# One fused attention block on one core: self attention's lead in another order, and one small exponential ahead of two leads

## The reference

```python
# layer 0: 8 heads of 40, keys and values from 1020 context rows, and a small extra attention
out = (mha(x @ Wq, enc @ Wk, enc @ Wv) + ca_hs2) @ Wout + b_out + x
# layer 1: 20 heads of 16
h1 = ln(x);  x = attn(h1, h1)      @ o1_w + o1_b + x     # self attention, 512 keys
h2 = ln(x);  x = attn(h2, context) @ o2_w + o2_b + x     # cross attention, 1024 keys
h3 = ln(x);  a, g = split(h3 @ ff_w1 + ff_b1);  x = a * gelu(g) @ ff_w2 + ff_b2 + x
# attn: softmax(q k^T * scale) v, exact to fp32, with the row's maximum taken off first
```

## Time and profile before

| | us |
|---|---|
| median of 3 runs | 864.62 |
| lowest and highest | 861.23 to 865.34 |
| the profiled execution, its own time | 866.39 |
| its span, first to last instruction | 864.6 |
| self attention's lead, first maximum on PE to first scores | 315.85 to 342.97 |

### The profile page before, as it was taken

How to read it: one execution, slowest core, us unless ns; L and a number is a source line. 1 busy time by engine, 2 the same in 40 slices (tenths; PEclk the granted TensorE clock), 3 DMA queues, 4 the chain that set the end, 5 groups by cost and what they waited for, 6 DMA issues and landing times.

```text
span 864.6 us, 11612 instructions
## 1 busy us (share of the span) xinstructions
PE 813.4 (94%) x4172; PEld 448.9 (52%) x4172; DVE 585.0 (68%) x1104; ACT 488.0 (56%) x744; POOL 121.4 (14%) x201
## 2 busy tenths in 40 slices
PE   5899999999999998999999889999999999899998
PEld 3777644444466665333335553333333333678888
DVE  4454576777685547599966468999999962684231
ACT  4643454554543632576777676777667777863130
POOL 5100103100005342000004500000000000540000
PEclk9998999999999998599999959999999999999999
DMA  8986478522301184122116512222222000500000
GB/s 289 283 280 212 135 219 258 149 85 67 122 15 57 33 258 131 53 75 69 45 35 114 161 37 42 53 50 53 47 53 41 2 2 24 236 1 1 31 0 31
DMA packets 30966, 83.18 MB, mean 96 GB/s; under 512 B 5172, under 2 KB 9212, under 8 KB 28606
## 3 DMA queue, kind: packets, MB, share of 16 engines
q1 hardware_dynamic: 30110, 79.71, 32.1%
q0 software_dynamic: 800, 2.73, 0.9%
HBM read 56.12 MB, written 25.89 MB: 95 GB/s over the span
## 4 chain that ended last, share of the span: by engine, by line
PE 72%; DVE 12%; DMA 7%; ACT 5%; issue 4%; SPq 0%; POOL 0%; ACTq 0%; POOLq 0%; DVEq 0%
PE PS L1002 20%; PE PS L945 15%; PE PS L623 10%; PE PS L1629 8%; PE PS L982 7%; DVE maxp L1137 5%; PE PS L1647 4%; DVE negm L1137 3%; PE PS L1448 2%; DMA k_d<-split 2%; ACT probs L1097 2%; DMA w_raw<-in_ff_w 1%; DVE turned L1182 1%; DMA q_sl<-msplit 1%; DMA w_v<-in_Wv 1%
## 5 line engine op out<-in xcount | busy, mean ns | idle before, releaser
L1097 ACT ACTIVATE probs<-PS 128x1024 f32<-128x1024 f32 (+1 forms) x336 | 310.5, 971 | 139.8 <-PE PS L982 136.8
L1137 DVE TENSOR_REDUCE maxp<-PS 128x1 f32<-128x512 f32 (+1 forms) x400 | 251.5, 678 | 43.1 <-PE PS L945 42.1
L945 PE MATMUL PS<-k_sl,q_sl 48*128 48x512 f32 (+2 forms) x592 | 225.8, 456 | 9.9 <-DVE maxp L1137 2.0
L982 PE MATMUL PS<-q_sl,k_sl 50*128 50x512 f32 (+3 forms) x672 | 204.1, 435 | 8.5 <-ACT probs L1097 6.0
L945 PEld LDWEIGHTS PS<-k_sl,q_sl 48*128 48x128 f32 (+2 forms) x592 | 103.3, 190 | 168.4 <-DVE maxp L1137 105.4
L1137 DVE TENSOR_REDUCE negm<-PS 128x1 f32<-128x512 f32 (+1 forms) x192 | 121.5, 677 | 28.5 <-PE PS L945 27.8
L982 PEld LDWEIGHTS PS<-q_sl,k_sl 50*128 50x128 f32 (+2 forms) x672 | 103.1, 192 | 54.6 <-ACT probs L1097 25.4
L1002 PE MATMUL PS<-probs,v2c 128*32 128x512 f32 x640 | 87.4, 616 | 1.0
L665 DVE TENSOR_TENSOR split<-PS,split 128x512 fp32r<-128x512 f32 (+3 forms) x54 | 34.8, 649 | 54.9 <-ACT split L640 54.5
L1002 PE MATMUL PS<-probs,v0c 128*64 128x512 f32 (+1 forms) x256 | 62.0, 605 | 0.0
L640 ACT CAST split<-PS 128x512 fp32r<-128x512 f32 (+3 forms) x54 | 29.8, 554 | 51.8 <-PE PS L623 38.5
(11 more groups left out here) (195 smaller groups left out, 1099.7 us busy)
## 6 DMA issues: line engine op xcount, KB each, us to landing
k_d<-split SPq DMA_DIRECT2D x20, 512.0 KB, 4.0
q_d<-split SPq DMA_DIRECT2D x12, 512.0 KB, 4.1
k_sl<-k_d SPq DMA_DIRECT2D x8, 640.0 KB
k_sl<-k_d SPq DMA_DIRECT2D x40, 128.0 KB, 5.7
q_sl<-q_d SPq DMA_DIRECT2D x40, 128.0 KB
k_sl<-k_d SPq DMA_DIRECT2D x20, 256.0 KB, 5.4
w_raw<-in_ff_w SPq DMA_DIRECT2D x1, 3840.0 KB, 12.9
k_sl<-k_d SPq DMA_DIRECT2D x8, 320.0 KB
```

Of the source, the lines that this page charges most:

```text
L945: nc.tensor.matmul(PS[0:a.qt, SBANKS[k % 3], 0:cn], q_view(g)[f:f + a.rows, j // a.stack, q * a.qt:(q + 1) * a.qt], k_view(g)[f:f + a.rows ...
L982: mm = nc.tensor.matmul(PS[0:sz, 2 * (x % 2) + half, 0:a.nq], k_view(g)[f:f + a.rows + 2, j // a.stack, t * 128:t * 128 + sz], q_view(g)[f ...
L1097: nc.scalar.activation(probs[0:a.size[t], x % PRING, :, 0:a.nq], PS[0:a.size[t], 2 * (x % 2):2 * (x % 2) + 2, 0:a.nq], ACT.Exp, scale=a.sc ...
L1137: nc.vector.tensor_reduce((maxp if nch > 1 else negm)[0:a.qt, g.turn, o:o + 1], PS[0:a.qt, SBANKS[k % 3], 0:a.chunks[c][1]], AX.X, ALU.max ...
```

## The change

A table `SELF_LEAD` sets the order of the self lead slot by slot: each pair says how many side products come, and how many maxima behind them. It begins with three products and no maximum, goes on with one product and two or three maxima, and ends with three maxima. A helper `self_lead` cuts products and maxima along it, and the three engines follow it instead of `share`. The flip comes at the end of the slot that completes the chunk. Besides, ACT does one exponential of one column (`warm`) before the self attention and before the cross attention; its result is not used. POOL's and SP's queues are not changed.

```diff
@@ -569,7 +570,16 @@
-    self_side = Side(alternate(selfp, selfp.jobs[2 * KF:], selfv, selfv.jobs), A_SELF.lead - 1, 1)
+    self_side = Side(alternate(selfp, selfp.jobs[2 * KF:], selfv, selfv.jobs), A_SELF.lead)
+    SELF_LEAD = ((3, 0), (1, 2), (1, 2), (1, 3), (1, 2), (1, 2)) + 6 * ((1, 3),) + ((0, 3),)
+
+    def self_lead(st):
+
+        jobs, per = iter(self_side.jobs), st.groups[0].a.per_step
+        items = iter([(c, i, m) for c in range(st.lead) for i, m in st.chunk(c)[1]])
+        slots = [([next(jobs) for _ in range(nj)], [next(items) for _ in range(ni)]) for nj, ni in SELF_LEAD]
+        assert next(jobs, None) is None and next(items, None) is None
+        return [(j, n, [c for c, i, m in n if m % per == per - 1]) for j, n in slots]
@@ -1005,18 +1015,17 @@
-        for x in range(st.lead):
+        for jobs, items, whole in self_lead(st) if side is self_side else []:
+            for ph, j in jobs:
+                pe_projection(pe, ph, [j])
+            for _, i, m in items:
+                item(i, m)
+            flips(whole)
+        for x in range(0 if side is self_side else st.lead):
...
-            elif side is self_side:
-                among = 2 if x else 0
-                for n, (ph, j) in enumerate(side.share(x)):
-                    pe_projection(pe, ph, [j])
-                    maxima([x], among * n, among * (n + 1))
-                maxima([x], among * len(side.share(x)))
-                flips([x])
@@ -1193,20 +1206,14 @@
+        for jobs, items, _ in self_lead(st) if side is self_side else []:
+            for _, i, m in items:
+                reduce(i, m)
+            for ph, j in jobs:
+                dve_projection(dve, ph, [j])
@@ -1778,10 +1785,12 @@
             act.wait_ge(v1_set, 1)
+            nc.scalar.activation(warm[:, :], eps[:, :], ACT.Exp)
             act_attention(act, S_SELF, side=self_side)
...
             act_join(act, join1, cross_in, crossp)
+            nc.scalar.activation(warm[:, :], eps[:, :], ACT.Exp)
             act_attention(act, S_CROSS)
```

More of the change, by code:

```diff
@@ L260, in build @@
     eps = place("eps", [128, 1])
+    warm = place("warm", [128, 1])
     ca_raw = place("ca_raw", [128, 2, 8 * KF])
@@ L1070, in flipped @@
                                    PS[0:2 * a.cols, flip_bank(st, i), 0:a.qt]).then_inc(st.flipped, 1)
-        for c in range(st.lead):
+        for jobs, _, whole in self_lead(st) if side is self_side else []:
+            for ph, j in jobs:
+                act_projection(act, ph, [j])
+            flipped(whole)
+        for c in range(0 if side is self_side else st.lead):
             if side is not None:
```

## The result

| | before | changed |
|---|---|---|
| median, 20 executions each | 865.64 us (861.23 to 872.11) | 858.55 us (853.79 to 863.86) |
| ratio, 95% interval | | 0.992 (0.990 to 0.994) |
| profiled execution: own time / span | 866.39 / 864.6 us | 860.27 / 858.5 us |
| its mean granted clock | 0.964 | 0.974 |

The forecast was 859.4.

The account below looks back on a forecast made before the run. PE was taken as the main bound (72% of the chain), with both table loads on the path. Lead -2.3, exponentials -2.56 and clock -0.3 sum to -5.2 us, from a median of 864.62 to 859.4; range 854.0 to 863.5.

Parts of the forecast that it names:

- The start: Self lead's start: two maxima behind s8 instead of four, 0.43 us for 2.49, so -2.06 us.
- Third maxima and waits: Self lead's middle: a third maximum in the seven slots v1 to v7, +1.54 us; waits for banks and flip, +0.65.
- The end: Self lead's end: six maxima behind v7 instead of ten, 2.65 us against 5.08, so -2.43 us.
- The lead in all: Self lead, start, middle and end summed: -2.3 us, scores starting near 340.7; bounds -3.0 to -1.1.
- The rival in which the lead gains nothing: Each slot loses its 0.18 us of play and the end waits anyway; only table loads remain, -2.6, 862.0; 15%.
- The two exponentials: Ahead of self and cross attention: each takes a 1.28 us table load off the path, -2.56 us; bounds -3.0 to 0.
- The drain rival: A drain of 1.38 us lay hidden before each table load, so 1.6 us more go, 857.8; 3%.
- direct terms: The forecast without its clock term: the lead's -2.3 us and the two exponentials' -2.56 us.
- The clock: Scores starting at 340.7 may still run at 2.4 GHz instead of half clock: -0.3 us, bounds 0 to -0.5.
- The clock stays up: Rival: PE's clock does not fall around self's scores, or returns steps earlier; up to 5.9 us more go, 855; 20%.
- The clock falls inside the lead: Rival: PE's clock halves among the self lead's slots, nearly doubling their cost; slower, 867; 7%.
- Group 3's load: Does not move; its maxima are first wanted in self's fifth step, with cover at least 4 us thick, so no wait.

Follow-up runs that it names:

- e1: Changed kernel without its two small exponentials, so the new order of the lead alone; median 861.02 us, ratio 0.996 to before.
- e2: Kernel before with nothing but the two small exponentials added; median 860.98 us, ratio 0.996 to before.
- e11: Kernel before with the one-column exponential added ahead of self attention alone; median 860.16 us, ratio 0.995 to before.
- e12: Kernel before with the one-column exponential added ahead of cross attention alone; median 864.22 us, ratio 1.000 to before.
- e4: Changed kernel with six unread matmuls added in PE's idle times at self attention's start; median 858.57 us, ratio 0.993 to before.
- e6: Changed kernel with unread matmuls at self's and cross's starts and a table that removes the flip's wait; median 854.35 us, ratio 0.986 to before.
- e9: e6's kernel word for word, run again; median 853.97 us, ratio 0.989 to before.
- e10: Changed kernel with the table that removes the flip's wait and unread matmuls at self's start, none in cross's; median 853.48 us, ratio 0.986 to before.
- e8: Kernel before with unread matmuls added at self attention's start alone; median 864.61 us, ratio 0.999 to before.
- e3: Changed kernel with another lead table that puts the flip into a slot without a third maximum; median 859.73 us, ratio 0.995 to before.
- e5: Changed kernel with unread matmuls added in cross attention's lead; median 860.49 us, ratio 0.994 to before.

## Why the prediction was right, step by step

**The start**, -2.06: shown, s9 0.43 us behind the first maximum.

**Third maxima and waits**, +1.54 and +0.65. Slots of 2.02 to 2.05 us confirm the 0.22 of a third maximum, but the sum counts one too many: v7's third maximum is among the seven slots and again among the six maxima of the end. Six slots make it +1.3. The waits were undersized. The flip waited 0.64 for a forecast of 0.55, and its slot was 0.7 longer than one without a wait; bank waits came twice, 0.25 us each, where the hand-run queues gave one of 0.1. Together they are +1.2 for +0.65.

**The end**, -2.43: 2.70 us for 5.08, -2.38.

**The lead in all**: -2.0 for -2.3 (the terms as measured give -1.9), in two traces of the changed kernel and in e1 (25.13, 25.18, 25.19), -1.9 ± 0.4 in e1's time at equal clock. The maximum that was counted twice hid part of the missed waits. The rival in which the lead gains nothing is refuted: PE waited in three slots, not in all.

**The two exponentials**, -2.56: -1.28 at each place in e2, e11 and e12, and -2.5 ± 0.4 in e2's time at equal clock. `lifted` was not delayed. The drain rival is refuted: it would have made the two exponentials worth 4.2 us (2.56 and its 1.6), four standard errors from what e2 gave. Nor is there room for a drain ahead of the old load: it started 1.11 us behind the first scores (342.97 to 344.08), and in e2, without a load there, the exponential itself started 1.12 behind them (343.06 to 344.18). The new loads start 0.02 us behind a busy engine, and the small exponentials 0.01 to 0.02 behind the load. The Trainium skill, page "ScalarE: Activation LUTs", section "What ACT_TABLE_LOAD costs", has a load of 1283 ns, with which the 1.28 us agree, and a drain of 1380 ns, which this case doesn't show at either place.

**Both together.** At equal clock the changed kernel is 3.65 ± 0.38 us faster, and e1 and e2 add up to 4.4 ± 0.6. My direct terms came to -4.9. The traces' own stretches give -4.6 (2.0 and twice 1.28). So the terms were somewhat large, by the lead's 0.3 and by a rest of up to 0.9 that the traces don't place and that may lie in the correction by the clock.

**The clock**, -0.3: this is the term that was mis-sized. The mean granted clock rose from 0.9703 to 0.9750 over 80 and 31 executions, and by the slope that is 2.2 us (error 0.6). The scores did not even run at full clock in the first trace (half from 341.56, scores at 341.59). What shrank is the stretch behind them: 12.9 us of steps at half clock for 16.5, which is 1.3 us of the profiled execution's gain. The means differ by 5.9 us: 3.65 at equal clock and 2.2 with the clock. The first set's 7.1 and the second's 4.1 in the medians lie on either side.

**The number.** That 859.4 lies 0.9 from the median of 858.55 is in part luck. The direct terms were 1.2 us too large and the clock's 1.9 too small, and the start value, the median of three runs of before (864.62), lay 1.0 under the median of twenty (865.64).

**The clock stays up**, 20%: neither trace of the changed kernel shows it. e4, e6, e9 and e10 do at self attention's start, and its price in the trace was right: "up to 5.9" was forecast, and 144.75 less 138.73 is 6.0. In the time e6 and e9 reached the rival's 855; e4 did not, and e10 is left open. That order can raise the clock is suggested by e1 (0.9758 in 12 executions) but not shown: e2 and e11 lie as far apart (0.9725 and 0.9780), and only an exponential in cross attention tells them apart.

**The clock falls inside the lead**, 7%: not among the side products in any of the nine traces with the new order; once in e2, one of five with the old order, for 3.4 us. It fell there behind the four maxima and their wait of 1.34 us at the lead's start, a wait that the prediction took for harmless. The Trainium skill, page "TensorE: Matmul & The Clock Gate", section "A second HAM failure mode: psum-queue depth-cycling", blames short idles between groups. The fall at 341.16 before agrees, behind maxima with waits of PE under 0.6 us. e8's at 344.83 came with no idle in the profile, though with matmuls at half their pace. The clock also stayed at half through windows in which PE was busy for all of 5.00 us (the changed kernel's 350 to 355 above).

**Group 3's load**: the steps wait for nothing new near 361; the stretches of all kernels without half clock agree to 0.07 us.

## What to carry to other kernels

Where a load of an activation table stands on the path, look for a hole of 1.5 us on ACT ahead of it: a one-column activation there buys the whole load, and the trace before tells this exactly. Alternate work that keeps PE busy with work at DVE's pace, in slots whose sum on PE just exceeds DVE's, and look for what needs the result of a slot at once (here the flip). When changes of half a per cent are compared, read the mean granted clock of each execution beside its time: it went with most of the spread here, and at equal clock the apparent gains of 4 us of one exponential and of 0 of its twin became 1.5 and 1.0.

## What the runs showed of the hardware beyond the forecast

- What a us at half clock costs is reproducible: 0.37 us in self attention's steps (6.0 us for 16.5), and 0.27 on average over the kernel, an estimate from the slope (4.7 us for 0.01 of mean clock, which is 17.2 us at half clock). Where the clock falls is not.
- The clock can fall with no idle of PE in the profile (e8 at 344.83). There maxima and unread matmuls of 512 columns took turns and started 0.43 us apart at full clock, against 0.22 for maxima in a row.
- The changed kernel's two traces had half clock for 17.1 and 13.7 us at self's start and for 17.1 and 30.7 at cross's.
- A one-column exponential took 0.20 us (a square root of that size 0.30).
- Matmuls that nobody reads can go with a higher clock and a shorter time (e6 and e9, with e3's table: 0.986 and 0.989 of before), and can eat their gain where PE has no real hole (e8: 0.999). At one place alone they did not beat the changed kernel (e4 858.57, e5 860.49).
